# Decoder layers on one core: the first row maxima of three attention layers are taken in the preceding projection stage

## The reference

```python
q, k, v = split(x @ Wq + bq), split(src @ Wk + bk), split(src @ Wv + bv)
scores = einsum('bhqd,bhkd->bhqk', q, k) / sqrt(16)      # + slopes and causal mask in L3_attn
out = einsum('bhqk,bhkd->bhqd', softmax(scores), v) @ Wo + bo
```

## Time and profile before

| | |
|---|---|
| median of 3 runs | 5066.7 us (5058.59 to 5066.75) |
| span of the profiled execution | 5059.4 us |
| PE busy | 4179.5 us, 83% |
| DVE busy | 2848.1 us, 56% |
| ScalarE busy | 2373.1 us, 47% |
| POOL busy | 1483.3 us, 29% |
| projection stages of l1x, l2a, l3a, first load to end | 1446.5 to 1537.7, 2318.7 to 2374.5, 4020.1 to 4079.8 us |
| DMA, mean | 96 GB/s |

### The profile page before, as it was taken

How to read it: one execution, slowest core, us unless ns; L and a number is a source line. 1 busy time by engine, 2 the same in 40 slices (tenths; PEclk the granted TensorE clock), 3 DMA queues, 4 the chain that set the end, 5 groups by cost and what they waited for, 6 DMA issues and landing times. The chain is left out here.

```text
span 5059.4 us, 69705 instructions
## 1 busy us (share of the span) xinstructions
PE 4179.5 (83%) x20292; PEld 1977.2 (39%) x20292; DVE 2848.1 (56%) x6426; ACT 2373.1 (47%) x4593; POOL 1483.3 (29%) x1306
## 2 busy tenths in 40 slices
PE   7669766689678996897969799999997988089986
PEld 5322355377443332573334233333335644012223
DVE  3448473501566884004860387878863265298866
ACT  4337431243233775232743354545541245269992
POOL 3111131212130111112220288778880223200111
PEclk9669987799887998897989899999997989579998
DMA  7656212354033332674323311211201144633421
GB/s 249 129 104 120 48 49 34 118 201 147 29 133 56 65 61 64 242 235 126 84 69 148 117 61 60 74 60 59 74 28 45 36 107 86 193 63 90 93 54 37
DMA packets 374291, 486.70 MB, mean 96 GB/s; under 512 B 84772, under 2 KB 288020, under 8 KB 360516
## 3 DMA queue, kind: packets, MB, share of 16 engines
q1 hardware_dynamic: 366528, 447.77, 31.9%
q0 software_dynamic: 6384, 32.61, 2.1%
q10 hardware_dynamic: 1068, 2.66, 0.2%
HBM read 325.07 MB, written 143.92 MB: 93 GB/s over the span
## 5 line engine op out<-in xcount | busy, mean ns | idle before, releaser
L1251 POOL TENSOR_TENSOR lc_totals<-lc_totals,lc_weights 128x1024 f32<-128x1024 f32 (+1 forms) x320 | 623.3, 1948 | 165.1 <-DVE lc_totals L1200 134.1
L1160 ACT ACTIVATE lc_weights<-ps 128x1024 f32<-128x1024 f32 x384 | 393.6, 1025 | 441.0 <-PE ps L1077 430.0
L1181 DVE TENSOR_REDUCE lc_part_max<-ps 128x2 f32<-128x1024 f32 x384 | 466.1, 1214 | 200.5 <-PE ps L1057 199.0
L1077 PE MATMUL ps<-lc_q,lc_k 64*128 64x512 f32 x1536 | 397.3, 596 | 0.0
L1087 PE MATMUL ps<-lc_weights,lc_v 128*64 128x512 f32 x1536 | 372.2, 605 | 0.0
L773 DVE TENSOR_REDUCE l1x_core_part_max<-ps 128x1 f32<-128x512 f32 x512 | 316.4, 681 | 72.5 <-PE ps L597 72.4
L769 DVE CUSTOM_DVE_ANT_0 l3x_core_unused<-ps,l3x_core_mask_q 128x512 f32<-128x512 f32 x512 | 330.7, 686 | 6.4 <-DVE l3x_core_row_max L777 4.9
L732 ACT ACTIVATE l3x_core_weights<-ps 128x512 f32<-128x512 f32 x512 | 327.5, 694 | 7.8 <-PE ps L665 7.3
L732 ACT ACTIVATE l1x_core_weights<-ps 128x512 f32<-128x512 f32 x512 | 266.1, 602 | 84.0 <-PE ps L665 83.8
L715 ACT ACTIVATE ps<-l3x_core_mask_k 128x512 f32<-128x512 f32 x384 | 270.4, 704 | 32.9 <-DMA l3x_core_mask_k<-in_mask_k 32.9
L597 PE MATMUL ps<-l3x_core_k,l3x_core_q 96*128 96x512 bf16 x512 | 214.7, 420 | 54.0 <-DVE l3x_core_part_max L769 38.9
(11 more groups left out here) (477 smaller groups left out, 8558.9 us busy)
## 6 DMA issues: line engine op xcount, KB each, us to landing
cf_w<-in_L1f_w SPq DMA_DIRECT2D x32, 1024.0 KB, 7.2
lc_k<-latent_k SPq DMA_DIRECT2D x32, 768.0 KB, 6.6
lc_v<-latent_values SPq DMA_DIRECT2D x32, 768.0 KB, 5.1
k_parts<-proj_parts SPq DMA_DIRECT2D x56, 384.0 KB, 2.8
latent_k<-feed_staged SPq DMA_DIRECT2D x64, 256.0 KB, 2.3
latent_values<-feed_staged SPq DMA_DIRECT2D x64, 256.0 KB, 2.0
q_parts<-proj_parts SPq DMA_DIRECT2D x40, 384.0 KB, 2.9
q_parts<-proj_parts SPq DMA_DIRECT2D x40, 256.0 KB, 3.0
```

The source lines that it names most:

```text
L1077: mm = nc.tensor.matmul(out[j], k_tile[g % RING][strip(j), i * P:(i + 1) * P], q_tile[g % RING][strip(j), :], start=False, stop=True)
L1160: nc.scalar.activation(weights[:, i % TILES, :, :], k.ps[:, B0 + (i % 2) * HEADS:B0 + (i % 2 + 1) * HEADS, 0:nq], ACT.Exp, scale=scale).th ...
L1181: nc.vector.reduce_max(own, k.ps[:, A0:A0 + HEADS, :], AX).then_inc(a_taken, 1)
L1251: nc.gpsimd.tensor_tensor(total, total, own, ALU.add).then_inc(added_by_pool, 1)
```

## The change

A new class, `FirstMaxima`, holds the stacks of q and k of groups 0 and 1 of batch 0 (`q_pair`, `k_pair`) and their maxima across both stages. The order of the split units changes: q unit 0, then the k units that hold the first 128 channels of batch 0 (two in l1x, one in the others), then the other q units, then the other k units. When the stores of split `FIRST_SPLITS + 1` are issued (split 4 in l1x, 3 in the others), SP waits for the stores of the splits 0 to `FIRST_SPLITS - 1` and issues eight loads of the parts of both groups. From unit 11 on PE computes one chunk behind each split unit and two behind each kept unit, and DVE takes its maximum, 64, 32 and 32 chunks in all. The chunks have three PSUM banks, and the units five in place of eight. The rows of ones and the slopes for these groups are loaded at the start of the projection stage. In the core stage the loads of groups 0 and 1, their rows of ones and both pass_a are gone; it begins with turn(0, 0). The load of ctxT is cut in two: batch 0 with a wait at unit 1, and the rest with a wait at unit 12. The other users of `project_stage` keep their order.

```diff
--- before.py
+++ after.py
@@ project_stage
-def project_stage(k, units, weights, stores=(), late=(), late_unit=0, prefetch=()):
+def project_stage(k, units, weights, stores=(), late=(), prefetch=(), first=None):
...
+    BANKS = 8 if first is None else first.BANK
+    late_at = {n: i for i, (n, _) in enumerate(late)}
+    beside = {} if first is None else first.beside(units)
...
+            if first is not None:
+                first.load_constants(sync)
             for tile, source in prefetch:
...
                     for destination, taken in part_stores(unit[4], parts[:, i % 3, :, 0:unit[2]]):
                         sync.dma_start(destination, taken).then_inc(parts_stored[i % 3], 16)
+                    if first is not None and i == first.FIRST_SPLITS + 1:
+                        for r in range(first.FIRST_SPLITS):
+                            sync.wait_ge(parts_stored[r], stored_by[r])
+                        first.load_parts(sync)
                     i += 1
...
-                if n >= 8:
-                    pe.wait_ge(evacuated, n - 7)
+                if n >= BANKS:
+                    pe.wait_ge(evacuated, n - BANKS + 1)
...
                 last.then_inc(ready, 1)
+                if n in beside:
+                    first.tensor(pe, beside[n])
...
+            for n in range(len(units)):
+                if n in splits:
+                    part_remainder(splits.index(n), n)
+                if n in beside:
+                    first.vector(dve, beside[n])
+            if first is not None:
+                first.finish(dve)
@@ attention_stage
+        if maxima_made is not None:
+            q_stack = [maxima_made.q_of(r) for r in range(2)] + [sb(f"q{r}", [rows_b, heads, nq], BF16)[:] for r in range(2, RING)]
+            k_stack = [maxima_made.k_of(r) for r in range(2)] + [sb(f"k{r}", [rows_b, heads, nk], BF16)[:] for r in range(2, RING)]
...
+        own_rings = range(0 if maxima_made is None else 2, RING)
+        n_ones = len(own_rings) * (2 if causal else 1)
...
             for g in range(2):
-                load_group(0, g)
+                if maxima_made is None:
+                    load_group(0, g)
+                else:
+                    sync.sem_inc(loaded[g], 16 * n_loads)
...
-            pass_a(0, 0, range(NCH))
-            turn(0, 0)
-            pass_a(0, 1, range(NCH))
+            if maxima_made is None:
+                pass_a(0, 0, range(NCH))
+                turn(0, 0)
+                pass_a(0, 1, range(NCH))
+            else:
+                pe.sem_inc(a_ready, 2 * (NCH + 1))
+                turn(0, 0)
...
-            for r in range(RING if small else 0):
+            for r in own_rings if small else ():
...
+            else:
+                dve.sem_inc(a_taken, 2 * (NCH + 1))
+                negate(0, 0)
@@ new
+class FirstMaxima:
+    BANK, BANKS = 5, 3
+    def __init__(self, k, held, name, q_store, k_store, nq, nk, slopes=None):
+        nc = k.nc
+        self.k, self.nq, self.nk, self.slopes = k, nq, nk, slopes
+        self.wide = min(BANK, nk)
+        self.nwide, nqt = nk // self.wide, nq // P
+        self.rows_a = STACK + (3 if slopes is not None else 0)
+        self.FIRST_SPLITS = 1 + self.nwide
+        self.chunks = [(g, qi, j, c) for g in range(2) for qi in range(nqt) for j in range(HG) for c in range(self.nwide)]
+        self.q_pair = held.enter_context(nc.sbuf_tensor(f"{name}_q_pair", [self.rows_a + 3, 2 * HG, nq], BF16))
+        self.k_pair = held.enter_context(nc.sbuf_tensor(f"{name}_k_pair", [self.rows_a + 3, 2 * HG, nk], BF16))
+        self.part_max = held.enter_context(nc.sbuf_tensor(f"{name}_part_max", [P, 2, HG * nqt, self.nwide], F32))
+        self.row_max = held.enter_context(nc.sbuf_tensor(f"{name}_row_max", [P, 2, HG * nqt], F32))
+        own = slice(0, 2 * HG * HD)
+        self.parts = (stack_loads(self.q_pair, pick(q_store, own, slice(0, nq))) + stack_loads(self.k_pair, pick(k_store, own, slice(0, nk))))
...
+    def q_of(self, r):
+        return self.q_pair[:, r * HG:(r + 1) * HG, :]
+    def k_of(self, r):
+        return self.k_pair[:, r * HG:(r + 1) * HG, :]
+    def beside(self, units):
+        START = 11
+        out, left = {}, len(self.chunks)
+        for n in range(START, len(units)):
+            some = left if n == len(units) - 1 else min(left, 1 if units[n][0] == "split" else 2)
+            if some:
+                out[n] = some
+            left -= some
+        return out
+    def load_constants(self, sync):
+        for tile, source in self.constants:
+            sync.dma_start(tile, source).then_inc(self.k.first_loaded, 16)
+    def load_parts(self, sync):
+        for tile, source in self.parts:
+            sync.dma_start(tile, source).then_inc(self.k.first_loaded, 16)
+    def keys_of(self, qi, c):
+        return slice(c * self.wide, (c + 1) * self.wide) if self.slopes is None else slice(0, (qi + 1) * P)
+    def tensor(self, pe, count):
+        k, nc = self.k, self.k.nc
+        for n in range(self.by_tensor, self.by_tensor + count):
+            g, qi, j, c = self.chunks[n]
+            if n == 0:
+                pe.wait_ge(k.first_loaded, self.loads_before + 16 * (len(self.parts) + len(self.constants)))
+            if n >= self.BANKS:
+                pe.wait_ge(k.first_taken, self.chunks_before + n - self.BANKS + 1)
+            keys, qs = self.keys_of(qi, c), slice(qi * P, (qi + 1) * P)
+            out = k.ps[:, self.BANK + n % self.BANKS, 0:keys.stop - keys.start]
+            mm = nc.tensor.matmul(out, self.q_pair[0:self.rows_a, g * HG + j, qs], self.k_pair[0:self.rows_a, g * HG + j, keys],
+                                  start=True, stop=self.slopes is None)
+            if self.slopes is not None:
+                mm = nc.tensor.matmul(out[:, qs], k.ident_bf[:, :], k.above_q[:, :], start=False, stop=True)
+            mm.then_inc(k.first_ready, 1)
+        self.by_tensor += count
+    def vector(self, dve, count):
+        k, nc = self.k, self.k.nc
+        for n in range(self.by_vector, self.by_vector + count):
+            g, qi, j, c = self.chunks[n]
+            slot, keys = j * (self.nq // P) + qi, self.keys_of(qi, c)
+            out = self.part_max[:, g, slot, c:c + 1] if self.nwide > 1 else self.row_max[:, g, slot:slot + 1]
+            dve.wait_ge(k.first_ready, self.chunks_before + n + 1)
+            nc.vector.reduce_max(out, k.ps[:, self.BANK + n % self.BANKS, 0:keys.stop - keys.start], AX).then_inc(k.first_taken, 1)
+        self.by_vector += count
+    def finish(self, dve):
+        if self.nwide > 1:
+            dve.wait_ge(self.k.first_taken, self.chunks_before + len(self.chunks))
+            self.k.nc.vector.reduce_max(self.row_max[:], self.part_max[:], AX)
@@ self_or_cross_attention
+        first = FirstMaxima(k, held, name, q_parts, k_parts, S, nk, slopes)
...
-                late = [(ctxT[:], inp["ctxT"])]
+                late = [(1, [(ctxT[:, :, 0:nk], inp["ctxT"][:, :, 0:nk])]), (1 + nk // BANK, [(ctxT[:, :, nk:], inp["ctxT"][:, :, nk:])])]
...
+            ahead = CH * nk // BANK
+            units = q_units[0:1] + k_units[0:ahead:CH] + q_units[1:]
+            units += [u for n, u in enumerate(k_units) if n >= ahead or n % CH]
+            if late:
+                late[1] = (len(q_units) + nk // BANK + ahead // CH, late[1][1])
+            project_stage(k, units + kept_units(lambda c, t: source[:, c, t * P:(t + 1) * P], w[:, :, 2 * C:], values), loads,
+                          late=late, prefetch=prefetch, first=first)
```

More of the change, by code:

```diff
@@ L154, in _ @@
                 unit = units[n]
-                if late and n == late_unit:
-                    pe.wait_ge(late_in, 16 * len(late))
-                if n >= 8:
-                    pe.wait_ge(evacuated, n - 7)
+                if n in late_at:
+                    pe.wait_ge(late_in[late_at[n]], 16 * len(late[late_at[n]][1]))
+                if n >= BANKS:
+                    pe.wait_ge(evacuated, n - BANKS + 1)
                 rows = P if unit[0] == "split" else unit[2]
                 for cols, lhsT, rhs, start, stop in unit[1]:
-                    last = nc.tensor.matmul(k.ps[0:rows, n % 8, cols], lhsT, rhs, start=start, stop=stop)
+                    last = nc.tensor.matmul(k.ps[0:rows, n % BANKS, cols], lhsT, rhs, start=start, stop=stop)
                 last.then_inc(ready, 1)
+                if n in beside:
+                    first.tensor(pe, beside[n])
         @block.scalar
@@ L178, in _ @@
                 if unit[0] == "given":
-                    if late and n == late_unit:
-                        act.wait_ge(late_in, 16 * len(late))
+                    if n in late_at:
+                        act.wait_ge(late_in[late_at[n]], 16 * len(late[late_at[n]][1]))
                     if i >= 3:
@@ L214, in _, with part_remainder @@
                 nc.vector.memset(value[:], 1.0).then_inc(ones_set, 1)
-            for i, n in enumerate(splits):
+            def part_remainder(i, n):
```

(12 more changed lines are left out.)

61 lines of the change are left out of this document (36 added, 25 removed).

## The result

The median is 5082.4 us (5075.3 to 5088.1, 7 runs) against 5066.8 us (5058.6 to 5077.6, 7 runs) for the kernel before: ratio 1.0032, 95% interval 1.0023 to 1.0042. The profiled execution has a span of 5080.8 us against 5059.4, 21.4 more. The change costs 15.7 us by the medians and 21.4 by the profiled spans; the forecast was 8.4.

A forecast was written before the change was run, and what follows sets the result against it. Core-stage prologues were bound by first loads, then DVE's maxima; split phases by a ring waiting for stores, then PE. 28.5 + 4 + 35 - 59.1 = +8.4 us gave span 5067.8, 5075.1 in the median's terms, range 5050 to 5090.

The forecast's parts named there:

- slower (over 10 us): Whole kernel: outcome more than 10 us slower than before, given 0.39.
- (a): Projection stages: loads run at the stores' rate, 337 GB/s at full share; stalls 13, time 5060; chance 0.10.
- (c): Split phase: DVE decides, each maximum lengthens the ring's period; 14 in place of 4, +18, 5085; chance 0.15 with (e).
- (d): Behind the last split: PE keeps its lead, the tail costs only the products, 21; -6, 5061; chance 0.05.
- Gains, 59.1: Core stages: shorter prologues save 34.5, 14.8 and 9.3, PE's wait saves 3, l3a's half clock costs 2.5; bounds 54 and 63.
- Tail, 35: Behind the last split: more kept units left plus the maxima's products add 35 us; bounds 21 and 40.
- a shorter cold start: Tail: PE idles less beforehand, so 4.5 us were taken off for the three layers.
- Maxima among the splits, 4: Split phase: one 0.60 us maximum behind each of 23 splits, two of three covered, adds 4 us; bounds 0 and 14.
- (e): Core stage: first group still waits long, for the ones or loads; gains fall by 10; chance 0.15 with (c).
- The stores behind the loads, 28.5: Split phase: stores wait behind part loads on SP's queue, 12.5 us in l1x, 8 each in l2a and l3a; bounds 0, 33.
- (b): Split phase: stores don't wait for the loads, 0 in place of 28.5; -20, 5047, faster; chance 0.18.

The follow-up runs named there:

- the row edit: Changed kernel with the core stage's first row of maxima issued ahead of the loads of group 3: 5072.2 us, ratio 1.0010 to the kernel before.
- the short reductions: Changed kernel with each early maximum in l1x and l2a reading only 128 of 512 columns, products whole: 5080.6 us, ratio 1.0026 to the kernel before.
- the kernel with the loads at the last splits: Changed kernel with part loads behind the fourth split from the end, first early product at the third kept unit: 5092.7 us, ratio 1.0051 to the kernel before.
- the kernel with single loads: Changed kernel with one part load behind each split's stores over eight splits, first early product two units later: 5073.9 us, ratio 1.0011 to the kernel before.
- the one with six slots: Changed kernel with six slots of parts in place of three in the projection stages: 5025.2 us, ratio 0.9911 to the kernel before.
- the best placing of loads and row: Changed kernel with part loads cut by group, spread over splits, a gate per group, and row ahead of group 3's loads: 5046.8 us, ratio 0.9965.

## Why the prediction was right, and where it was not

The forecast was 5075.1 with a range of 5050 to 5090; the time is 5082.4, inside, and the sign was the forecast's. The 15.7 us lie in what the prediction called slower (over 10 us), to which it gave 0.39. The range is wide: it holds the rivals (a), (c) and (d) as well, so it is the steps that tell. And a part of the nearness is luck: the forecast was moved from the span to the median by 7.3 us, the difference in the kernel before, and in the changed kernel that difference is 1.6. By the spans the forecast is 13.0 us too low, by the medians 7.3. By its own steps:

**Gains, 59.1.** Of these 58.6 stand in the prologues, where the table has 60.1; the other two, +3 for PE's wait behind the first product and -2.5 for l3a's half clock, lie behind the table's last mark. The wait of 1.01 us is gone from l1x, and l3a's first products run at half clock (0.61 us); what the two come to was not measured. The first products come 16.4, 11.1 and 12.3 us after the stage's start, against 15.5, 12.3 and 13.5. That the row stands behind the loads of groups 2 and 3 is shown by the row edit in l1x, 6.0 us. In l2a and l3a the row's DMAs are issued 7.9 and 9.1 us after the start, where 8.6 and 10.0 were forecast, but taking the row ahead of group 3 gave only 1.5 and 1.4 us: another wait, at the transpose, is close behind.

**Tail, 35.** Measured 38.4. The kept unit takes the 1.30 us of the sum and TensorE sets it, shown by the short reductions. Without the 4.5 us that I took off for a shorter cold start the sum is 39.6. That term was the error: in l1x the granted clock is still 0.50 from 1537 to 1541, at the start of the tail, and in the kernel before it is 0.54 and 0.61 from 1515 to 1519. The cold start was not shorter.

**Maxima among the splits, 4.** From the twelfth cast to the last subtraction l1x and l2a took about 1.8 and 0.9 us more, l3a 2.3 less, 0.5 in all. The casts with a maximum between them come 2.50 us apart in l1x, not the 2.9 of (c), and the gains did not fall by 10 as in (e).

**The stores behind the loads, 28.5.** This is the mis-sized term: 41.1 us up to the twelfth cast (19.0, 11.5, 10.6 against 12.5, 8, 8). The mechanism was there, a gap in DVE's casts right behind the loads, ended by a store. Of the 12.6 us too few, the rate accounts for 3.5 + 2.4 + 2.4 = 8.3 by an estimate: I charged 172 GB/s from the earlier trace rows, and the loads move 137 in l1x of the kernel with the loads at the last splits, while no engine works; in l1x of the changed kernel they move 114 to 134. What the other 4 are is not shown. A candidate is the second hold, PE's own wait of 19.6 us for the loads at unit 11, behind which the projection's products stand, at half clock afterwards. The prediction did not name that wait, though the change adds it. In the kernel with single loads, and in the one with six slots, ScalarE waits for PE behind it (9.5 and 16.1 us in one piece).

**The rivals.** (a), loads at 337 GB/s, is excluded by 137. (b), no wait at all: excluded by the 41.1 us and by the gap of 17.9 us that a store ends. (c) and (e): see above. (d): the tail is 38.4, not 21. The Trainium skill's 341 GB/s for 1 MB to 128 partitions (DMA: Bandwidth & Descriptors, section Bandwidth), cited with the prediction, is two and a half times the 137 that these loads moved; here the measurement decides.

Errors of the terms (stores, tail, maxima, gains in the prologues): +12.6, +3.4, -3.5 and -1.5, together +11.0. The forecast within the table's marks is 28.5 + 4 + 35 - 58.6 = +8.9, and with the errors 19.9, as the table has it.

## What to carry to other kernels

Work moved into a stage that looks half idle takes its loads with it: ask first which store or load of that stage will be behind them, how many buffers stand between it and the engine, and what is queued behind the engine that waits for the data. Before moving anything into a stage whose idle time is a ring's latency, try more slots in the ring: here, on top of the change, they gave 57 us, and the best placing of loads and row gave 36. If loads must go there, spread them at the pace of the stores and let each consumer wait for its own part alone; the two together, with the loads cut by group, gave 23 us here, and what each gives alone is not shown.

## What was not expected of the hardware

- The loads of the stacks moved 137 GB/s at a DMA share of 1.08 while no engine worked, and the loads of the same kind in the core stage of the kernel before 172 at 0.98. Those are cut by group; cut so in the projection stage, they moved 134 to 157 GB/s in stretches of 4 us. The cause of the difference is open.
- Stores that land in 2.8 us took far longer beside the loads, and less so from another queue. DMA issues from 1475 to 1500 (count, KB each, median us from issue to landing), first the changed kernel, then the one with the loads on ScalarE's queue:

```profile
q_parts<-proj_parts SPq DMA_DIRECT2D x4, 384.0 KB, 16.0
...
q_parts<-proj_parts SPq DMA_DIRECT2D x3, 256.0 KB, 17.6
```

```profile
q_parts<-proj_parts SPq DMA_DIRECT2D x5, 384.0 KB, 8.9
q_parts<-proj_parts SPq DMA_DIRECT2D x6, 256.0 KB, 8.8
```

A queue of their own did not protect the stores, but their landing takes about half as long. That kernel also spreads the loads over four splits, so how much of the half is the queue is not shown.
